# q and k in two f16 parts on the row halves of TensorE, and one exponential for both scores of a head pair

## The reference, cut to what matters

```python
NUM_HEAD = 16; SCALE = 8.0; d = D // NUM_HEAD          # d = 8
q = (x @ Wq + bq).reshape(B * NUM_HEAD, -1, d)         # the same for k and v
attn = softmax(einsum('bqd,bkd->bqk', q, k) * SCALE, axis=-1)
ctx = einsum('bqk,bkd->bqd', attn, v).reshape(B, S, D)
```

## Time and profile before

| quantity | value |
|---|---|
| median of three runs | 1485.85 us |
| the profiled execution, its own time | 1489.87 us |
| its span in the profile | 1488.1 us |
| TensorE busy | 1327.0 us, 89% |
| VectorE busy | 1055.6 us, 71% |
| ScalarE busy | 949.4 us, 64% |
| GpSimd busy | 882.5 us, 59% |
| attention, preparation: to the first exponential | 79.1 us |
| attention loop: first to last exponential | 79.1 to 588.8 us |
| mixture phase: from about | 612 us to the end |
| mean granted clock of TensorE | 0.957 |

### The profile page before, as it was taken

How to read it: one execution, slowest core, us unless ns; L and a number is a source line. 1 busy time by engine, 2 the same in 40 slices (tenths; PEclk the granted TensorE clock), 3 DMA queues, 4 the chain that set the end, 5 groups by cost and what they waited for, 6 DMA issues and landing times. The chain is left out here.

```text
span 1488.1 us, 23328 instructions
## 1 busy us (share of the span) xinstructions
PE 1327.0 (89%) x6176; PEld 525.4 (35%) x6176; DVE 1055.6 (71%) x1843; ACT 949.4 (64%) x1732; POOL 882.5 (59%) x835
## 2 busy tenths in 40 slices
PE   2499898989889897599999999998999999999998
PEld 1223232322222221234444444443433444444443
DVE  6687887879787783577786786788878555455554
ACT  0055565757566576467767767766666777877776
POOL 2414342433433235467777777777777888878886
PEclk9997897989998899799999999999999999999999
DMA  2541523324252400431101001021110110001100
GB/s 60 86 68 41 78 56 57 74 38 91 35 83 51 65 5 9 124 94 29 40 9 40 27 29 40 8 85 34 57 37 8 37 29 26 13 21 29 30 7 8
DMA packets 92275, 65.36 MB, mean 44 GB/s; under 512 B 35786, under 2 KB 85900, under 8 KB 92172
## 3 DMA queue, kind: packets, MB, share of 16 engines
q1 hardware_dynamic: 91812, 63.91, 20.2%
q10 hardware_dynamic: 360, 0.30, 0.1%
HBM read 43.87 MB, written 20.05 MB: 43 GB/s over the span
## 5 line engine op out<-in xcount | busy, mean ns | idle before, releaser
L1266 POOL TENSOR_TENSOR m_hidl<-m_hid,m_hidh 128x512 f16<-128x512 f32 x520 | 613.3, 1185 | 212.2 <-ACT m_hidh L1311 188.8
L1534 DVE TENSOR_TENSOR m_hid<-m_silu,m_c 128x512 f32<-128x512 f32 x512 | 347.5, 684 | 247.7 <-ACT m_silu L1318 193.2
L588 ACT ACTIVATE a_probs<-a_score 128x512 f32<-128x512 f32 x512 | 293.8, 597 | 195.1 <-PE a_score L666 188.5
L1318 ACT ACTIVATE m_silu<-m_h 128x512 f32<-128x512 f32 x520 | 309.1, 595 | 131.1 <-PE m_h L1417 126.2
L1311 ACT ACTIVATE m_hidh<-m_hid 128x512 f16<-128x512 f32 x520 | 324.2, 624 | 90.8 <-DVE m_hid L1534 89.7
L762 DVE TENSOR_REDUCE a_mx<-a_mxps 128x2 f32<-128x1024 f32 x256 | 306.9, 1215 | 75.7 <-PE a_mxps L657 75.1
L666 PE MATMUL a_score<-a_qstack,a_kstack 74*128 74x512 bf16 x512 | 208.6, 412 | 21.3 <-DMA a_qstack<-a_mT 14.4
L657 PE MATMUL a_mxps<-a_kstack,a_qstack 72*128 72x512 bf16 x512 | 173.4, 424 | 43.2 <-DMA a_kstack<-t_parts 31.2
L1415 PE MATMUL m_h<-m_xh,m_wuh 128*128 128x512 f16 x520 | 198.8, 382 | 12.2 <-DMA m_rw<-rw 12.2
L1397 PE MATMUL m_y<-m_hidh,m_wdh 128*128 128x512 f16 x520 | 198.8, 382 | 2.5 <-ACT m_gT L1332 1.7
L1417 PE MATMUL m_h<-m_xh,m_wul 128*128 128x512 f16 x520 | 198.7, 382 | 0.0
(11 more groups left out here) (186 smaller groups left out, 1295.5 us busy)
## 6 DMA issues: line engine op xcount, KB each, us to landing
a_qstack<-t_parts SPq DMA_DIRECT2D x63, 128.0 KB
a_kstack<-t_parts SPq DMA_DIRECT2D x63, 128.0 KB
m_raw<-up SPq DMA_DIRECT2D x8, 512.0 KB, 3.9
m_raw<-down SPq DMA_DIRECT2D x8, 512.0 KB, 4.0
m_sT<-t_s SPq DMA_DIRECT2D x16, 256.0 KB, 3.4
t_parts<-a_qparts SPq DMA_DIRECT2D x24, 128.0 KB, 2.2
t_parts<-a_kparts SPq DMA_DIRECT2D x24, 128.0 KB, 2.3
a_xin<-x SPq DMA_DIRECT2D x8, 256.0 KB, 3.4
```

What stands on the lines that cost most here:

```text
L588: act.activation(probs[:, kt % 2, g, :], score[:, g % 2, :], ACT.Exp, scale=SCALE).then_inc(exp_done, 1)
L1266: pool.tensor_tensor(hidl[0:r0, k % r, :], hid[0:r0, k % r, :], hidh[0:r0, k % r, :], ALU.subtract).then_inc(lo_done, 1)
L1318: act.activation(silu[0:rows(q), k % RING[s.layer], :], hps[0:rows(q), k % 2, :], ACT.Silu, scale=1.0 / WS).then_inc(silu_done, 1)
L1534: dve.tensor_tensor(hid[:, k % r, :], silu[:, k % r, :], cps[:, (q // UPC[s.layer]) % 2, :], ALU.mult).then_inc(mul_done, 1)
```

## The change

q and k are scaled by 16 (weights and biases, `scaled_weights`, `bias_rows`) and held as two f16 parts. All four products of parts are stacked: 4 x 8 = 32 rows. One more row is constant (`ZROWS` = 33), and two carry the maximum over 1024 against 1024 (`KROWS` = 35). The stack has two halves: groups of even g start at partition 0, those of odd g at partition 64 (`HALF`), so a score or a maxima matmul works on one row half of TensorE. Both scores of a pair (g0 and g1, g2 and g3) are issued back to back into the two banks, and one exponential of 1024 columns takes both; the next pair waits for it. GpSimd has one instruction for a side in place of three. The stack is filled by eight loads for each stage into 16 partitions each, and stored by six stores of another shape (four for q, since its parts are stored twice, two for k). `max_rows` issues eight DMAs of half the size. `one_rows` becomes `constant_rows`, with four memsets in place of one for each of the two stacks.

```diff
-TERMS = [(a, b) for a in range(3) for b in range(3)]
-ROWS = DH * len(TERMS)
-MROW = ROWS
-KROWS = MROW + 2
+QS = 16.0
+MS = 1024.0
+HALF = P // 2
+ROWS = 4 * DH
+ZROWS = ROWS + 1
+KROWS = ZROWS + 2
...
-        STACK_LOADS = 2 * len(TERMS)
+        STACK_LOADS = 2 * 2 * 2
+        STORES = (4, 2)
...
+        def stack_load(eng, n, side, a, e, tiles, done):
+            r = HALF * e + 2 * DH * a
+            into = stack[side][n.p][r:r + 2 * DH, :, :, tiles].rearrange("r k h n x -> r (k h) (n x)")
+            there = scratch["kparts"][n.p] if side else scratch["qparts"][n.p, a]
+            eng.dma_start(into, there.rearrange("u j k (h e) x -> e (u j) (k h) x", e=2)[
+                e, :, :, tiles.start * P:tiles.stop * P]).then_inc(done, 16)
...
-                for a in range(3):
-                    sp.dma_start(scratch["parts"][n.p, side, a].rearrange("n p x -> p n x"),
-                                 parts[side][:, a, :].rearrange("p (n x) -> p n x", n=TILES)
-                                 ).then_inc(parts_out[side], 16)
+                for a in range(2):
+                    for u in range(1 if side else 2):
+                        there = scratch["kparts"][n.p, a] if side else scratch["qparts"][n.p, a, u]
+                        sp.dma_start(there.rearrange("j k g x -> g (j k) x"), parts[side][:, a, :]
+                                     ).then_inc(parts_out[side], 16)
...
                 for q in range(CH // KT):
-                    sp.dma_start(stack[0][where.p][MROW:KROWS, at].rearrange(
-                        "a g (k q t) -> a (g k) q t", k=KT, t=GT)[:, :, q, :], mT[GT * q:GT * q + GT]
-                        ).then_inc(m_in, 16)
+                    for e in range(2):
+                        r, c = HALF * e + ZROWS, GT * q + GT // 2 * e
+                        sp.dma_start(stack[0][where.p][r:r + 2, :, :, at, GT * q:GT * q + GT].rearrange(
+                            "a k h t -> a (k h) t"), mT[c:c + GT // 2]).then_inc(m_in, 16)
...
-                    for g in range(NG):
-                        act.wait_ge(score_full, s.at(64, 16 * tau + 4 * kt + g + 1))
-                        if g == 0 and not (s.first() and 4 * tau + kt < 2):
+                    for h in range(NG // 2):
+                        act.wait_ge(score_full, s.at(64, 16 * tau + 4 * kt + 2 * h + 2))
+                        if h == 0 and not (s.first() and 4 * tau + kt < 2):
 
                             act.wait_ge(pv_done, s.at(16, 4 * tau + kt - 1))
-                        act.activation(probs[:, kt % 2, g, :], score[:, g % 2, :], ACT.Exp, scale=SCALE
-                                       ).then_inc(exp_done, 1)
+                        act.activation(probs[:, kt % 2, 2 * h:2 * h + 2, :], score[:], ACT.Exp,
+                                       scale=SCALE / (QS * QS)).then_inc(exp_done, 2)
...
-                    pe.wait_ge(exp_done, s.at(64, 16 * tau + 4 * kt + g - 1))
-                pe.matmul(score[:, g % 2, :], stack[1][s.p][0:KROWS, tau, g, kt * P:kt * P + P],
-                          stack[0][s.p][0:KROWS, tau, g, :], start=True, stop=True
+                    pe.wait_ge(exp_done, s.at(64, 16 * tau + 4 * kt + g - g % 2))
+                h, e = divmod(g, 2)
+                r = slice(HALF * e, HALF * e + KROWS)
+                pe.matmul(score[:, e, :], stack[1][s.p][r, kt, h, tau, :], stack[0][s.p][r, :, h, tau, :], start=True, stop=True
                           ).then_inc(score_full, 1)
...
-            def one_rows(p):
-
-                dve.memset(stack[1][p][64:KROWS], 1.0).then_inc(init[p], 1)
+            def constant_rows(p):
+
+                for side, value in enumerate((0.0, MS)):
+                    for e in range(2):
+                        dve.memset(stack[side][p][HALF * e + ROWS:HALF * e + KROWS], value).then_inc(init[p], 1)
```

More of the change, by code:

```diff
@@ L650, in maxima @@
                 if j == 0 and at == 0 and ahead:
+                    if s.first() and where.p:
+                        pe.wait_ge(init[1], 4)
                     pe.wait_ge(qk_in[where.p], where.own(16 * STACK_LOADS, 16 * STACK_LOADS))
@@ L653, in maxima @@
                     pe.wait_ge(mx_done, s.at(32, 8 * ahead + j - 1))
-                qt = j // 2
-                for k in range(2):
-                    g = 2 * (j % 2) + k
-                    op = pe.matmul(mxps[:, j % 2, k, :], stack[0][where.p][0:ROWS, at, g, qt * P:qt * P + P],
-                                   stack[1][where.p][0:ROWS, at, g, :], start=True, stop=True)
+                qt, h = j // 2, j % 2
+                for e in (1, 0):
+                    r = slice(HALF * e, HALF * e + ZROWS)
+                    op = pe.matmul(mxps[:, h, e, :], stack[0][where.p][r, qt, h, at, :],
+                                   stack[1][where.p][r, :, h, at, :], start=True, stop=True)
                 op.then_inc(mx_full, 1)
```

149 lines of the change are left out of this document (73 added, 76 removed).

## The result

The changed kernel took 1541.92 us (median of 1528.15, 1542.91, 1540.93 and 1553.1), the kernel before, on the same chip, 1484.05. The ratio is 1.0403, 95% interval 1.0345 to 1.046: slower by 4%. The forecast was 1426, faster by 4%.

What follows compares the result with a forecast made beforehand. VectorE was taken to bound full stages at 56 us: 84.5 + 59.5 + 5 x 56 + 50.5 + 49.3 + 6 = 529.8 us at loop end, 60 less, giving 1426 us; 8-in-10 range 1404 to 1480.

Steps and rivals of the forecast that it cites:

- Loads: Attention loop's stack loads: eight a stage, not 18, end in 12.5 us; TensorE's 6 us stall and low clock behind it go.
- rival 1: TensorE stays at the low clock in the loop: step 4.55 us, stage 78, 22 more per stage; chance 0.16.
- The sum: Preparation, eight loop stages and 6 us of late rows end the loop at 529.8, where 590 stood: 60 us less.
- ScalarE's other work: ScalarE in a loop step: other work, up to 0.6 us, fits the 0.48 us in which it waits.
- Rows of the maxima, stores: SP's queue: eight row DMAs take 5.4 us; stores of 2.0 us each make rows late, 1 us a stage, 6 in all.
- The step on ScalarE: Exponential of 1024 columns takes 1.03 us, a pair 1.51, a step 3.02, a stage of 16 steps 48.3.
- Row halves together: TensorE's two matmuls of a pair run side by side on row halves: 0.22 us a pair, not 0.44.
- rival 3: Row halves run in series on TensorE: a step is 3.7 us, +46 us, 1472; chance 0.11.
- Preparation: Ahead of the loop: longer memsets, scaled weights and bias, and row DMAs move the first score from 78.5 to 84.5 us.
- The exponential itself: ScalarE in the loop: one exponential of 1024 columns takes 1.03 us where two of 512 take 1.19.
- Letting VectorE bound the stage: Full loop stages: VectorE's 53.5 us of work exceeds the chain's 48.3, so it bounds; 56 us a stage taken.

Runs made afterwards that it cites:

- e10: Changed kernel with scores contracting over 64 rows in place of 35, nothing else, both waits kept: 1475.4 us, ratio 0.993.
- e5: Changed kernel with two waits removed (rows of tile 1 issued first, q and k taken a step later) and scores over 64 rows: 1436.1 us.
- e4: Kernel before, with only paired scores and one exponential of 1024 columns added: 1536.2 us, ratio 1.042.
- e13: Changed kernel without the two waits, scores over 64 rows, maxima over 62, exponentials of 512 columns in the old order: 1416.8 us, ratio 0.964.
- e18: Changed kernel without the two waits, scores over 64 rows, maxima over 62, pairs and exponential of 1024 columns kept: 1435.7 us, ratio 0.966.
- e12: Kernel before with half its rows, scores over 37 and maxima over 36, exponential's scale a thousandth: 1756.2 us, ratio 1.182.
- e1: Changed kernel with the second pair of maxima of each step issued three times (extra pairs of 33 rows): 1556.6 us, ratio 1.054.
- e7: Changed kernel with only ScalarE's take of q and k moved one step later: 1488.5 us, no ratio.
- e8: Changed kernel with only the rows of tile 1 issued ahead of the q and k loads in SP's queue: 1537.2 us, ratio 1.015.
- e2: Changed kernel with two waits removed: rows of tile 1 issued first, ScalarE takes q and k a step later: 1469.6 us, ratio 0.998.
- e17: Kernel before with 37 of 74 rows in the scores only, maxima whole, scale a thousandth: 1810.2 us, ratio 1.220.

## Why the prediction was wrong, step by step

The step that failed stands under *Loads*, "The stall and the low clock behind it go", and with it the weight of rival 1, 0.16. The stall went; the clock did not come back. I set against rival 1 that the last stage kept 1.00 with scores and products alone. It did, with scores of 74 rows; the change has 35. I took TensorE's activity for time and never asked how much of the array works in that time. The loss: 57 steps at 4.65 in place of 3.27 us is 79 us, of the 97 by which the last exponential is later than forecast (626.4 against 529.8). The waits and the longer pair, below, are what is left for the other 18 us; their shares were not measured apart.

A second step failed beside it. With the clock mostly restored and the waits in place (e10) the change takes 1475.4 us, still 49 above the forecast, and the two waits are 39 of them (e10 against e5). *Loads* goes on: "What is late next is the engines' own work." The sum had 6 us for late rows and nothing for ScalarE's take or for its stand at the loop's turn. *Loads* had also read one stage for all: the kernel before waited 20.4 us for `a_kstack`, but 14.4 more for rows of the maxima, and four of its seven falls began at such a wait or just behind it.

- *Rival 1's sizes were right.* A step at the low level: 4.55 forecast, 4.65 measured; a whole stage there: 78, and the first took 79.0. By its formula 45% at the low level gives 1426 + 0.45 x 8 x 22 = 1505. (The gain of 60 us is gone at 60 / 176 = 34% of the time, not at 38; nothing else hangs on it.)
- *The forecast's sizes were right where the clock was high.* e5, with the rows filled and two waits gone, has full stages of 56.1, 56.7, 60.5, 61.2 and 55.8 us behind the first (forecast 56) and 1436.1 us in all (forecast 1426). The two long ones lie on both sides of ScalarE's stand of 4.78 us, and the second has a clock of 0.86.
- *ScalarE's other work "falls into the 0.48 in which it waits"*: true of its length, wrong of its releaser. The take of q waits 3.15 us for VectorE, and with both banks under one exponential TensorE waits with it. This wait was not in the sum.
- *Rows of the maxima, stores*: eight DMAs 5.4 us forecast, 5.35 measured. The late rows of tile 1 were forecast at 1 us a stage, 6 in all; four waits came, of 2.68, 3.48, 2.77 and 1.98 us, 10.9 in all. That one queue makes them late was right. The reason was not: the forecast had SP held up by slow stores, and SP waited 0.8 us for a store in the whole loop. Its time went into issuing. How long a store took to land is not shown.
- *The step on ScalarE*: 1024 columns took 1.02 us (forecast 1.03). A pair took 1.60 and not 1.51, since the exponential starts 0.51 behind the pair and not 0.43: the last stage of e5 is 51.0 where 49.3 was forecast.
- *Row halves together* (against rival 3): right. e4 shows rival 3 in the flesh, steps of 3.75 (forecast 3.7).
- *Preparation*: first score at 84.05, forecast 84.5. Right within a microsecond.
- *The exponential itself* was booked as a saving of work; its price (18.9 us, e13 against e18) stood in no term. Letting VectorE bound the stage was right for three of the full stages and wrong for the first, the two at the loop's turn and the last.

## What to carry to other kernels

When a change makes TensorE's matmuls narrower in rows, price the loop at the low level first, and ask what share of the array works, not only how long the engine is busy; filling the rows of a half with zeros on one side cost TensorE no time and was worth 67 us here. Before two consumers' buffers are merged into one instruction, list every wait of the engine that runs it: each now stops the producer as well. Read the level from the duration of a matmul that occurs at both, and not from the clock column alone.

## What the hardware did that I had not expected

- Rows move the granted clock: 37 rows of 74 kept a loop of 778 us at the low level while TensorE was busy 775.99 of 777.30 us (e12), and zeros in 29 more rows of each half took the changed kernel's products from 809 to 668 ns (e10). Those rows add nothing to any score, so it is the rows addressed more than the results; they hold 1024 on the k side, and rows that are zero on both sides were not tried. Added work on few rows does not replace them (e1). How rows and time trade against each other stays open.
- With few rows and a wait left, the time of one kernel spreads from execution to execution: e7 by 57 us, e8 by 59, the changed kernel by 25; with 64 rows e10 by 9. Few rows alone need not do it: nine of e2's ten executions lie within 13 us.
- With exponentials of 1024 columns ScalarE stood 4.3 to 9.2 us where the hardware loop goes round, with 512 under 0.5. Why is open.
- The granted clock is recorded from its first rise on; ahead of it the column shows 1.00 whatever it was (178 us in the changed kernel, 880 us in e12).
- Matmuls of 37 and 72 rows in turn cost some 0.1 us for each change between them at the low level (e17 against e12).
